# Two heads' transposed scores to one exponential of 1024 columns, in an attention between two mixtures of experts

## The chip, the cores and the metric

The kernel runs on 1 core of one Trainium2 chip. The metric is the device time of one execution in microseconds (us); times are medians of several runs.

## The reference

The reference is one layer: half a mixture of experts, attention, half a mixture of experts, on x of 4 x 512 tokens with 512 channels. The change touches the attention alone. For every batch and each of 16 heads of 32 channels:

```python
Xn = (X - mu) * jax.lax.rsqrt(var + LN_EPS) * ln_w + ln_b
Q, K, V = jnp.split(jnp.einsum('bsd,df->bsf', Xn, W_in), 3, axis=-1)
Q, K = (_rope(Q), _rope(K))
scores = jnp.einsum('bhqd,bhkd->bhqk', Q, K) / jnp.sqrt(jnp.float32(Dh))
probs = jax.nn.softmax(scores, axis=-1)
ctx = jnp.einsum('bhqk,bhkd->bhqd', probs, V)
out = jnp.einsum('bsd,df->bsf', ctx, W_out) + X
```

## The kernel before

One program feeds five engines, each with its own instruction stream in order: TensorE (PE), ScalarE (ACT), VectorE (DVE), GpSimd (POOL) and the DMA queue of SyncE (SP). The first expert stage runs to about 430 us of the span, attention to about 950 us, the second expert stage to the end.

Attention goes in 16 units (u = 0 to 15), four heads of one batch each. A unit's scores are computed twice. The first time (`pe_scores`, L445) queries lie on the partitions, one matmul of 512 columns for each head and each 128 queries. VectorE takes the row maximum (L1062), ScalarE writes the exponential in place and sums it (`act_scores`, L722: an ACTIVATE and then a read of the accumulator). The logarithm of that sum (L728) less the maximum is transposed (L452), copied (L1080, L1082) and placed by DMA (`fill`, L1350) as two extra rows of the stacked operand `St`. The second time (`pe_expo`, L465) keys lie on the partitions, the two extra rows subtract the logarithm, and ScalarE's exponential (`act_expo`, L735) gives the finished weights PT, which `pe_weigh` (L477) multiplies with V, four heads side by side, for 128 keys at a time.

All engines walk the same written order: for each u from -2 to 16, sixteen steps j = 0 to 15. At step j of unit u, TensorE issues, in this order:

- the first scores of unit u + 1. `scores_at` puts one in each step from 0 to 13, but two (numbers 5 and 6) in step 5 and two (10 and 11) in step 9. They use banks 4, 5 and 7 in turn, so number n waits (`a_den`) until ScalarE has summed number n - 3.
- the transposed scores number j - 3 of unit u (at steps 0 to 2 numbers 13 to 15 of unit u - 1). They use banks 2 and 3 in turn, so number n waits (`a_exp`) for exponential n - 2.
- in steps 0 to 5 a third of a projection for unit u + 2 (L434, four matmuls); in steps 7 to 9 and 11 to 13, where a unit has them, thirds of a value tile (L420) or of an output tile (L491, units 4, 5, 8, 9, 12 and 13); at steps 10, 14, 15 and 6 of the next unit, the four weighings of unit u.

ScalarE at step j does the exponential of the transposed scores first, and then those of the first scores; after these a cast of the projection (L715) at steps 5 and 8, and a tile's affine (L706, four ACTIVATEs) at step 6 (at 10 too in units 0 and 1, at neither from unit 10 on). L465, L445, L434 and L420 take their operands as fp32r; L477, L491, L271 and the fills L525 take plain fp32.

Unit 15 has no next unit: its steps hold the transposes (L271) and the router matmuls (L279) of the second expert stage. Before `fill` of unit 15, SP waits until all 240 transposed scores of units 0 to 14 have been issued (`a_ST`), and then issues five loads of the second expert stage.

Of the kernel before, what the change touches and what calls it, by code (L numbers as in the profile page):

```python
# [10 lines left out]
ACT = mybir.ActivationFunctionType  # L11
# [6 lines left out]
S = 512  # L18
NH = 16
DH = 32  # L20
# [47 lines left out]
def macaron_kernel(nc, X_in, ln_w, ln_b, W_in, W_out, gate_w, bias, w_gate, w_up, w_down,  # L68
# [4 lines left out]
    with ExitStack() as ctx:  # L73
# [20 lines left out]
        def bank(i):  # L94
            return ps[i // 2][:, i % 2, :]
# [19 lines left out]
        St = [at("St", AT + 16 * KB * j, [98, 2, 4, S], F32R) for j in range(3)]  # L115
        xT = [at("xT", AT + 48 * KB + 8 * KB * j, [128, 4, S], F32R) for j in range(2)]
        V = [at("V", AT + 64 * KB + 8 * KB * j, [128, 4, D]) for j in range(2)]
        PT = [at("PT", AT + 80 * KB + 2 * KB * j, [128, S]) for j in range(NP)]
        Y1 = at("Y1", AT + 16 * KB, [128, NT, D])
        HL = at("HL", AT + 104 * KB, [128, 4, S], F32R)  # L120
        o = AW + 36 * KB
# [333 lines left out]
        def pe_expo(e, u, j):  # L455
            d, hl, kt = St[u % 3], j % 4, j // 4
            n = 16 * u + j
            if j == 0:
                for h in range(4):
                    e.wait_ge(s_st[u % 3][h], 48 * (u // 3 + 1))  # L460
                e.wait_ge(s_m[u % 3], 32 * (u // 3 + 1))
                e.wait_ge(a_ones, 3)
            if n >= 2:
                e.wait_ge(a_exp, n - 1)
            e.matmul(bank(2 + j % 2), d[0:98, 1, hl, 128 * kt:128 * kt + 128], d[0:98, 0, hl, :],  # L465
                     start=True, stop=True).then_inc(a_ST, 1)

        def pe_weigh(e, u, kt):
            b = u // 4
            e.wait_ge(a_V, 4 * b + kt + 1)  # L470
            if kt == 0 and u:
                e.wait_ge(a_dr, u)
            for hl in range(4):
                n = 16 * u + 4 * kt + hl
                h = 4 * (u % 4) + hl
                e.wait_ge(a_exp, n + 1)
                t = e.matmul(bank(6)[32 * hl:32 * hl + 32, :], V[b % 2][:, kt, DH * h:DH * h + DH], PT[n % NP][:, :],  # L477
                             start=(kt == 0), stop=(kt == 3), tile_position=(0, 32 * hl), skip_group_check=True)
            t.then_inc(a_pv, 1)

# [46 lines left out]
        def pe_attention(e):  # L527
            for i in range(4):
                pe_atile(e, i)
            for u in range(-2, NU + 1):  # L530
                now, nxt, far, back = 0 <= u < NU, 0 <= u + 1 < NU, 0 <= u + 2 < NU, 0 <= u - 1 < NU
                new, val = new_tiles(u), new_values(u)
                if u == NU:
                    pe_logits(e, f2, 11)
                for j in range(16):
                    if u == NU - 1 and 2 <= j < 14:
                        pe_tile(e, f2, j - 2)
                    if u == NU - 1 and 6 <= j:
                        for i in {14: (8, 9), 15: (10,)}.get(j, (j - 6,)):
                            pe_logits(e, f2, i)  # L540
                    if nxt:
                        for s in scores_at(j):
                            pe_scores(e, u + 1, s)
                    if now and j >= 3:
                        pe_expo(e, u, j - 3)
                    if back and j < 3:
                        pe_expo(e, u - 1, j + 13)
                    if far and j < 6:
                        pe_project(e, u + 2, j // 3, j % 3)
                    if u == NU - 2 and j < 8 or u == NU - 1 and j < 3:  # L550
                        pe_fill(e)
                        pe_fill(e)
                    if u == -2 and j in (8, 9):
                        for third in range(3):
                            pe_value(e, j - 8, third)
                    if u == -1 and 8 <= j < 14:
                        pe_value(e, (j - 2) // 3, (j - 2) % 3)
                    if back and j == 6:
                        pe_weigh(e, u - 1, 3)
                    if u == NU and j == 6:  # L560
                        e.wait_ge(a_exp, 16 * NU)
                        pe_shared_up(e, f2, 0, (0,))
                    if j in T_AT[:len(new)]:
                        pe_atile(e, new[T_AT.index(j)])
                    for h, at_ in ((0, FIRST), (1, SECOND)):
                        if j in at_:
                            third = at_.index(j)
                            if val is not None:
                                pe_value(e, val + h, third)
                            if result_of(u, h) is not None:  # L570
                                pe_result(e, result_of(u, h), ((0, 1), (2,), (3,))[third])
                    if now and j == 10:
                        pe_weigh(e, u, 0)
                    if now and j == 14:
                        pe_weigh(e, u, 1)
                    if now and j == 15:
                        pe_weigh(e, u, 2)
                    if nxt and j == 15:
                        pe_rows(e, u + 1)
                    if u == NU and j in (8, 10, 12, 14):  # L580
                        pe_result(e, u - 4 + (j - 8) // 2)
# [147 lines left out]

        def act_expo(e, u, j):  # L730
            n = 16 * u + j
            e.wait_ge(a_ST, n + 1)
            if n >= NP:
                e.wait_ge(a_pv, (n - NP) // 4 + 1)
            e.activation(PT[n % NP][:, :], bank(2 + j % 2), ACT.Exp).then_inc(a_exp, 1)  # L735

        def act_attention(e):
            e.preload_act_table(ACT.Sqrt)
# [3 lines left out]
            for u in range(-2, NU + 1):  # L742
                now, nxt, far, back = 0 <= u < NU, 0 <= u + 1 < NU, 0 <= u + 2 < NU, 0 <= u - 1 < NU
                new = new_tiles(u)
                for j in range(16):
                    if u == NU - 2 and j == 9:
                        act_root(e, f2, 0)
                    if u == NU - 1 and 2 <= j < 14:
                        act_tile(e, f2, j - 2)
                    if now and j >= 3:  # L750
                        act_expo(e, u, j - 3)
                    if back and j < 3:
                        act_expo(e, u - 1, j + 13)
                    if nxt:
                        for s in scores_at(j):
                            act_scores(e, u + 1, s)
                    if far and j in S_AT:
                        act_split(e, u + 2, S_AT.index(j))
                    if u == -2 and j == 9:
                        act_stats(e, 1)  # L760
                        e.preload_act_table_set("natural_log_exp_and_others")
                    if j in T_AT[:len(new)]:
                        act_atile(e, new[T_AT.index(j)])
                    if nxt and j == 14:
                        act_log(e, u + 1)
# [684 lines left out]
```

## Time and profile before

| | |
|---|---|
| median of 3 runs | 1369.07 us (1364.05 to 1369.32) |
| the profiled execution | 1369.51 us, its span 1367.7 us |
| TensorE's granted clock, mean | 0.946 of full speed |
| PE busy over the span | 1189.1 us (87%) |
| ACT busy over the span | 512.9 us (37%) |
| DVE busy over the span | 622.5 us (46%) |

The mean over the span hides the stages: ScalarE is nearly idle in the expert stages and busy in attention. What bears on the change is the stretch from 500 to 926 us, and in it the order of time on TensorE and ScalarE.

### The profile page before, as it was taken

The page shows a single profiled execution, that of the slowest core. Times are in us where ns is not written, and L with a number is a line of the kernel's source. Part 1 is how long each engine was busy: PE and PEld are TensorE (multiplying, and loading weights), DVE is VectorE, ACT ScalarE, POOL GpSimd, SP SyncE. Part 2 cuts the span into 40 slices and gives each one's busy share as a digit, 9 for nine tenths or more (in the row PEclk, how much of TensorE's full clock was granted, in tenths as well). Part 3 has the DMA queues.
Part 4 walks back from the last instruction along what each step waited for, and adds up shares of the span by engine and source line. Part 5 has one row for each costly group of instructions (what it writes and reads, how often), then busy time and mean ns, then how long its engine had stood idle before and what let it go on. Part 6 is the DMA issues. An engine that isn't in the chain of part 4 may idle for free.

```text
span 1367.7 us, 25752 instructions
## 1 busy us (share of the span) xinstructions
PE 1189.1 (87%) x10130; PEld 758.6 (55%) x10130; DVE 622.5 (46%) x1130; ACT 512.9 (37%) x1297; POOL 509.6 (37%) x413
## 2 busy tenths in 40 slices
PE   7998998888892678999999999889998998888980
PEld 5535766566671554665565565464336766665650
DVE  6993222122224767677777776613980212221220
ACT  3312111111111268888788788742122111111100
POOL 0123455455552933233234233000304555454544
PEclk9999999999996788999999999999998999999995
DMA  9996999999978844433534533232845999999957
GB/s 348 348 404 213 313 342 339 339 338 324 331 168 227 261 108 105 98 101 97 144 82 106 155 81 88 65 131 92 324 171 169 337 344 343 337 341 332 322 84 134
DMA packets 146200, 307.27 MB, mean 225 GB/s; under 512 B 17568, under 2 KB 50720, under 8 KB 146080
## 3 DMA queue, kind: packets, MB, share of 16 engines
q1 hardware_dynamic: 112960, 238.32, 51.8%
q0 software_dynamic: 23808, 57.69, 18.4%
q10 hardware_dynamic: 9312, 9.62, 2.1%
q8 instruction: 81, 1.33, 0.4%
q14 instruction: 39, 0.32, 0.1%
HBM read 222.47 MB, written 61.87 MB: 208 GB/s over the span
## 4 chain that ended last, share of the span: by engine, by line
PE 50%; DMA 27%; DVE 11%; ACT 4%; issue 3%; POOL 3%; SPq 1%; DVEq 0%; POOLq 0%; ACTq 0%
DMA ya_d<-osb,tok 10%; DMA out<-osb,tok 10%; PE ps L369 9%; PE ps L385 5%; PE ps L434 5%; DMA buf<-xn_d,tok 4%; PE ps L477 4%; PE ps L465 4%; PE ps L445 4%; PE ps L491 4%; PE ps L317 2%; PE ps L316 2%; PE ps L420 2%; DVE osb L993 2%; PE ps L279 2%
## 5 line engine op out<-in xcount | busy, mean ns | idle before, releaser
L369 PE MATMUL ps<-bufT,gu 128*64 128x96 f32 x6144 | 298.1, 259 | 0.0
L369 PEld LDWEIGHTS ps<-bufT,gu 128*64 128x64 f32 x6144 | 287.6, 175 | 9.1 <-issue 2.5
L993 DVE TENSOR_SCALAR osb<-ps,gt 96x512 f32<-96x512 f32 x128 | 94.0, 746 | 283.7 <-PE ps L385 70.8
L1062 DVE TENSOR_REDUCE Mx<-ps 128x1 f32<-128x512 f32 x256 | 170.5, 684 | 79.3 <-PE ps L445 78.7
L682 ACT COPY bufT<-ps 128x384 f32<-128x384 f32 x128 | 61.0, 478 | 352.7 <-PE ps L352 352.6
L722 ACT ACTIVATE ps<-ps,Mx 128x512 f32<-128x512 f32 x256 | 175.7, 689 | 36.3 <-DVE Mx L1062 35.5
L385 PE MATMUL ps<-wd,h 64*96 64x512 f32 x768 | 180.4, 602 | 3.2 <-DVE osb L993 3.2
L735 ACT ACTIVATE PT<-ps 128x512 f32<-128x512 f32 x256 | 159.4, 623 | 57.4 <-PE ps L465 55.5
L1182 POOL DMA_INDIRECT buf<-xn_d,tok x128 | 128.0, 1000 | 96.5 <-issue 61.6
L445 PE MATMUL ps<-St 96*128 96x512 f32 x256 | 118.8, 480 | 18.6 <-ACT ps L722 15.7
L465 PE MATMUL ps<-St 98*128 98x512 f32 x256 | 112.0, 438 | 12.5 <-DMA St<-mh 8.2
L986 DVE TENSOR_TENSOR h<-sg,ps 128x288 f32<-128x288 f32 x64 | 29.1, 454 | 204.7 <-PE ps L369 204.7
L352 PE MATMUL ps<-cst,buf 96*128 96x96 f32 x512 | 67.9, 263 | 60.4 <-DMA buf<-xn_d,tok 58.8
L434 PE MATMUL ps<-xT,wqk 128*128 128x512 f32 x384 | 110.2, 413 | 5.9 <-DVE xT L1033 5.9
L352 PEld LDWEIGHTS ps<-cst,buf 96*128 96x128 f32 x512 | 47.2, 143 | 116.6 <-DMA buf<-xn_d,tok 69.3
L1227 POOL TENSOR_TENSOR t<-t,rp 128x512 f32<-128x512 f32 x32 | 41.2, 1286 | 187.4 <-DVE t L1047 185.7
L385 PEld LDWEIGHTS ps<-wd,h 64*96 64x96 f32 x768 | 58.8, 159 | 77.6 <-issue 71.8
L434 PEld LDWEIGHTS ps<-xT,wqk 128*128 128x128 f32 x384 | 76.9, 201 | 24.1 <-DVE xT L1033 6.3
L1218 POOL DMA_INDIRECT out<-osb,tok x32 | 46.1, 1439 | 108.3 <-DVE osb L993 69.0
L445 PEld LDWEIGHTS ps<-St 96*128 96x128 f32 x256 | 49.7, 194 | 64.2 <-ACT ps L722 33.4
L1218 POOL DMA_INDIRECT ya_d<-osb,tok x32 | 46.2, 1443 | 100.1 <-DVE osb L993 63.9
L465 PEld LDWEIGHTS ps<-St 98*128 98x128 f32 x256 | 49.9, 195 | 47.2 <-issue 22.1
(149 smaller groups left out, 1481.7 us busy)
## 6 DMA issues: line engine op xcount, KB each, us to landing
gu<-in_L_ffn_w_gate SPq DMA_DIRECT2D x64, 768.0 KB, 13.2
gu<-in_L_ffn_w_up SPq DMA_DIRECT2D x64, 768.0 KB, 15.5
wd<-in_L_ffn_w_down SPq DMA_DIRECT2D x64, 768.0 KB, 18.4
St<-HL SPq DMA_DIRECT2D x192, 128.0 KB, 2.3
wqk<-wp_d SPq DMA_DIRECT2D x32, 512.0 KB, 5.2
xn_d<-XN SPq DMA_DIRECT2D x24, 256.0 KB, 3.6
X<-in_L_attn_X SPq DMA_DIRECT2D x4, 1024.0 KB, 10.7
ya_d<-X SPq DMA_DIRECT2D x4, 1024.0 KB, 18.4
```

What stands on the lines that cost most here:

```text
L352: t = e.transpose(bank(x % 2)[:, CAP * c:CAP * c + CAP], f.buf[x % NB][:, 128 * c:128 * c + 128], cst[0:CAP, C_ID:C_ID + CAP])
L369: t = e.matmul(bk[64 * k:64 * k + 64, CAP * j:CAP * j + CAP], gu[:, 2 * k + m, c, j:F:3], f.bufT[(2 * q + k) % 4][:, c, :], start=(c == 0) ...
L385: t = e.matmul(bank(4 + k)[0:CAP, :], f.h[q % 2][p, CAP * j:CAP * j + CAP], wd[p, j, :], start=(j == 0), stop=(j == 2), tile_position=(64 ...
L434: t = e.matmul(bk, wqk[:, x, c, k, :], xT[y][:, c, :], start=(n == 0), stop=(n == 11))
L445: e.matmul(bank((4, 5, 7)[n % 3]), d[0:96, 0, hl, 128 * qt:128 * qt + 128], d[0:96, 1, hl, :], start=True, stop=True).then_inc(a_sc, 1)
L465: e.matmul(bank(2 + j % 2), d[0:98, 1, hl, 128 * kt:128 * kt + 128], d[0:98, 0, hl, :], start=True, stop=True).then_inc(a_ST, 1)
L722: e.activation(bk, bk, ACT.Exp, bias=Mx[:, qt, hl:hl + 1], accum_out=Dn[:, qt, hl:hl + 1]).then_inc(a_den, 1)
L735: e.activation(PT[n % NP][:, :], bank(2 + j % 2), ACT.Exp).then_inc(a_exp, 1)
L993: e.tensor_scalar(f.osb[x % 4][:, :], bank(4 + x % 2)[0:CAP, :], f.gt[:, x % 8:x % 8 + 1], None, ALU.mult).then_inc(f_ev, 1)
L1062: e.tensor_reduce(Mx[:, qt, hl:hl + 1], bank((4, 5, 7)[n % 3]), AX, ALU.max, negate=True).then_inc(a_max, 1)
L1182: e.indirect_dma_start(out=f.buf[x % NB][:, :], out_offset=None, in_=f.xn_d, in_offset=bass.IndirectOffsetOnAxis(ap=f.tok[:, x:x + 1], axi ...
L1218: e.indirect_dma_start(out=f.y[x % 2], out_offset=bass.IndirectOffsetOnAxis(ap=f.tok[:, x:x + 1], axis=0), in_=f.osb[x % 4][:, :], in_offs ...
```

## The change

Transposed scores are made for two neighbouring heads at one step, into banks 2 and 3, which are the two halves of `ps[1]`, and one ACTIVATE of 1024 columns turns both into weights. PT becomes four buffers of two heads instead of eight of one. The pair (0, 1) stands at step 3, (2, 3) at 5, and so on to (12, 13) at 15 and (14, 15) at step 1 of the next unit; even steps have none. A pair's two matmuls wait (`a_exp`) until the exponential of the pair before has ended.

```diff
--- before.py
+++ after.py
@@ -115,7 +115,7 @@
         St = [at("St", AT + 16 * KB * j, [98, 2, 4, S], F32R) for j in range(3)]
         xT = [at("xT", AT + 48 * KB + 8 * KB * j, [128, 4, S], F32R) for j in range(2)]
         V = [at("V", AT + 64 * KB + 8 * KB * j, [128, 4, D]) for j in range(2)]
-        PT = [at("PT", AT + 80 * KB + 2 * KB * j, [128, S]) for j in range(NP)]
+        PT = [at("PT", AT + 80 * KB + 4 * KB * j, [128, 2, S]) for j in range(NP // 2)]
         Y1 = at("Y1", AT + 16 * KB, [128, NT, D])
         HL = at("HL", AT + 104 * KB, [128, 4, S], F32R)
         o = AW + 36 * KB
@@ -460,10 +460,11 @@
                     e.wait_ge(s_st[u % 3][h], 48 * (u // 3 + 1))
                 e.wait_ge(s_m[u % 3], 32 * (u // 3 + 1))
                 e.wait_ge(a_ones, 3)
-            if n >= 2:
-                e.wait_ge(a_exp, n - 1)
-            e.matmul(bank(2 + j % 2), d[0:98, 1, hl, 128 * kt:128 * kt + 128], d[0:98, 0, hl, :],
-                     start=True, stop=True).then_inc(a_ST, 1)
+            if n:
+                e.wait_ge(a_exp, n // 2)
+            for k in range(2):
+                e.matmul(ps[1][:, k, :], d[0:98, 1, hl + k, 128 * kt:128 * kt + 128], d[0:98, 0, hl + k, :],
+                         start=True, stop=True).then_inc(a_ST, 1)
 
         def pe_weigh(e, u, kt):
             b = u // 4
@@ -473,8 +474,8 @@
             for hl in range(4):
                 n = 16 * u + 4 * kt + hl
                 h = 4 * (u % 4) + hl
-                e.wait_ge(a_exp, n + 1)
-                t = e.matmul(bank(6)[32 * hl:32 * hl + 32, :], V[b % 2][:, kt, DH * h:DH * h + DH], PT[n % NP][:, :],
+                e.wait_ge(a_exp, n // 2 + 1)
+                t = e.matmul(bank(6)[32 * hl:32 * hl + 32, :], V[b % 2][:, kt, DH * h:DH * h + DH], PT[n % NP // 2][:, n % 2, :],
                              start=(kt == 0), stop=(kt == 3), tile_position=(0, 32 * hl), skip_group_check=True)
             t.then_inc(a_pv, 1)
 
@@ -541,10 +542,10 @@
                     if nxt:
                         for s in scores_at(j):
                             pe_scores(e, u + 1, s)
-                    if now and j >= 3:
+                    if now and j >= 3 and j % 2:
                         pe_expo(e, u, j - 3)
-                    if back and j < 3:
-                        pe_expo(e, u - 1, j + 13)
+                    if back and j == 1:
+                        pe_expo(e, u - 1, 14)
                     if far and j < 6:
                         pe_project(e, u + 2, j // 3, j % 3)
                     if u == NU - 2 and j < 8 or u == NU - 1 and j < 3:
@@ -558,7 +559,7 @@
                     if back and j == 6:
                         pe_weigh(e, u - 1, 3)
                     if u == NU and j == 6:
-                        e.wait_ge(a_exp, 16 * NU)
+                        e.wait_ge(a_exp, 8 * NU)
                         pe_shared_up(e, f2, 0, (0,))
                     if j in T_AT[:len(new)]:
                         pe_atile(e, new[T_AT.index(j)])
@@ -729,10 +730,10 @@
 
         def act_expo(e, u, j):
             n = 16 * u + j
-            e.wait_ge(a_ST, n + 1)
+            e.wait_ge(a_ST, n + 2)
             if n >= NP:
                 e.wait_ge(a_pv, (n - NP) // 4 + 1)
-            e.activation(PT[n % NP][:, :], bank(2 + j % 2), ACT.Exp).then_inc(a_exp, 1)
+            e.activation(PT[n % NP // 2][:, :, :], ps[1][:, :, :], ACT.Exp).then_inc(a_exp, 1)
 
         def act_attention(e):
             e.preload_act_table(ACT.Sqrt)
@@ -747,10 +748,10 @@
                         act_root(e, f2, 0)
                     if u == NU - 1 and 2 <= j < 14:
                         act_tile(e, f2, j - 2)
-                    if now and j >= 3:
+                    if now and j >= 3 and j % 2:
                         act_expo(e, u, j - 3)
-                    if back and j < 3:
-                        act_expo(e, u - 1, j + 13)
+                    if back and j == 1:
+                        act_expo(e, u - 1, 14)
                     if nxt:
                         for s in scores_at(j):
                             act_scores(e, u + 1, s)
```

## Rows read from the trace of the kernel before

**Rows 1.** Windows of the whole core: PE, PEld, DVE, ACT, POOL busy us (count), PEclk, DMA share, GB/s.
```profile
440.00:561.00 121.00, 93.25 (x351) 60.18 (x352) 83.50 (x152) 71.68 (x183) 59.71 (x48) 0.82 0.54 154
561.00:892.00 331.00, 320.90 (x1459) 190.46 (x1458) 231.17 (x405) 271.83 (x683) 96.46 (x78) 0.99 0.41 103
```
**Rows 2.** Waits from 561 to 892: who waited for whom, total us, times, longest us.
```profile
PEld ps L445 <- ACT ps L722: 21.3, 28, 1.6
...
PEld ps L465 <- ACT PT L735: 12.6, 18, 1.7
```
**Rows 3.** Groups by line: ScalarE's 1024-column form; busy us, mean ns | idle before, releaser.
```profile
L639 ACT ACTIVATE sgs<-ps 128x1024 f32<-128x1024 f32 x8 | 8.2, 1024 | 65.8 <-PE ps L304 65.8
```
**Rows 4.** Timeline, ScalarE, unit 2, steps 5 to 8: start us, us, operation.
```profile
560.21 0.60 ACT L735 ACTIVATE PT<-ps 128x512 f32<-128x512 f32 x1
560.71 0.66 ACT L722 ACTIVATE ps<-ps,Mx 128x512 f32<-128x512 f32 x1
...
565.07 0.65 ACT L735 ACTIVATE PT<-ps 128x512 f32<-128x512 f32 x1
565.54 0.72 ACT L722 ACTIVATE ps<-ps,Mx 128x512 f32<-128x512 f32 x1
566.12 0.26 ACT L722 ACTIVATION_READ_ACCUMULATOR ps<-ps,Mx 128x1 f32 x1
```
**Rows 5.** Timeline, TensorE, unit 2: step 5 unstalled, step 9 stalled.
```profile
559.31 0.63 PE L445 MATMUL ps<-St 96*128 96x512 f32 x2
...
565.88 1.04 PE L445 MATMUL ps<-St 96*128 96x512 f32 x2
...
566.43 0.19 PEld L445 LDWEIGHTS ps<-St 96*128 96x128 f32 x1 [0.59 <-ACT ps L722]
```
**Rows 6.** Timeline, step 9 of units 4 and 13: the sum read, the second weight load.
```profile
616.33 0.27 ACT L722 ACTIVATION_READ_ACCUMULATOR ps<-ps,Mx 128x1 f32 x1
...
616.82 0.19 PEld L445 LDWEIGHTS ps<-St 96*128 96x128 f32 x1 [0.24 <-ACT ps L722]
...
847.51 0.24 ACT L722 ACTIVATION_READ_ACCUMULATOR ps<-ps,Mx 128x1 f32 x1
...
848.89 0.19 PEld L445 LDWEIGHTS ps<-St 96*128 96x128 f32 x1 [0.24 <-issue]
```
**Rows 7.** Timeline, unit 6: ScalarE late at step 5, TensorE stalled at step 9.
```profile
663.98 0.59 ACT L735 ACTIVATE PT<-ps 128x512 f32<-128x512 f32 x1
...
670.18 0.50 PE L445 MATMUL ps<-St 96*128 96x512 f32 x1 [0.49 <-ACT ps L722]
```
**Rows 8.** Timeline, TensorE, unit 5, steps 13 to 15.
```profile
650.48 1.02 PE L491 MATMUL ps<-wout,cT 128*128 128x512 f32 x2
650.94 0.80 PE L465 MATMUL ps<-St 98*128 98x512 f32 x1
651.67 1.06 PE L477 MATMUL ps<-PT,V 128*32 128x512 f32 x8
```
**Rows 9.** Timeline, unit 15, first steps: TensorE and SP's queue.
```profile
888.75 0.60 PE L465 MATMUL ps<-St 98*128 98x512 f32 x1
...
890.47 0.47 PE L465 MATMUL ps<-St 98*128 98x512 f32 x1
...
893.46 1.23 SPq L1350 DMA_DIRECT2D St<-mh  x2
...
897.73 0.77 PE L465 MATMUL ps<-St 98*128 98x512 f32 x1 [4.91 <-DMA St<-mh]
```
**Rows 10.** Timeline, units 15 and 16: the last exponentials and the last weighing.
```profile
914.67 0.48 PE L465 MATMUL ps<-St 98*128 98x512 f32 x1
914.99 0.60 PE L271 MATMUL ps<-cst,XN 128*128 128x128 f32 x4
...
922.88 0.71 PE L465 MATMUL ps<-St 98*128 98x512 f32 x2
...
925.22 0.14 PEld L477 LDWEIGHTS ps<-PT,V 128*32 128x32 f32 x2 [0.56 <-ACT PT L735]
```

## The prediction

> **What bounds the kernel now.** I read the busy windows first, then the waits, then the timelines of TensorE and ScalarE step by step. In the 331 us in which attention runs steadily, TensorE is busy 320.9 us at a granted share of 0.99, ScalarE 271.8 us [rows 1]. Two fp32r matmuls of 512 columns in a row take 0.63 us where a single one takes 0.40 [rows 5], so TensorE takes a new one every 0.23 us; the reader is to see that it is nearly always fed. Its waits are small: 21.3 us for ScalarE's sums of the first scores, 12.6 us put down to the exponentials PT [rows 2]. So ScalarE's total, 59 us short of the stretch, is not what sets the end; what counts is when it releases something to TensorE. One place stands out: step 9, where two first scores are issued. The second of them, number 11, needs the sum of number 8, which ScalarE makes at step 7. In unit 2 the two matmuls span 1.04 us instead of 0.63, 0.41 us of stall; the sum's read ends at 566.38, and the second one's weights load from 566.43 [rows 4, 5]. The same place stalls 0.49 us in unit 6 [rows 7].
>
> **ScalarE's saving.** It gives up 256 exponentials of 512 columns (0.60 us, as at 560.21) for 128 of 1024. In a row a single one lets the next instruction start after 0.50 or 0.47 us (560.21 to 560.71, 565.07 to 565.54) [rows 4]. The 1024-column form exists elsewhere in the kernel and takes 1.024 us, 0.42 more than 0.60 [rows 3, 4]. So a pair occupies about 0.48 + 0.42 = 0.90 us against 0.96 for two: 0.06 saved, 128 x 0.06 = 7.7 us in all. As TensorE is the full engine, I cost this gain at nothing, with 7.7 us as its other bound (a rival below). The Trainium skill ("ScalarE: Activation LUTs", section "What ACT_TABLE_LOAD costs") gives an ACTIVATE a fixed 186 ns, of which 93 ns overlap back to back. By that the saving would be 93 ns a pair, an estimate of 11.9 us in all; the rows here show two thirds of it.
>
> **Step 9, the main cost.** What ScalarE does from step 5 until the sum of score 8 changes order. Before: exponential 2, scores 5 and 6, cast, exponential 3, score 7, the affine, exponential 4, score 8. After: pair (2, 3), scores 5 and 6, cast, score 7, affine, pair (4, 5), score 8. Exponential 5 is now ahead of score 8. Two pairs (1.80) stand for three singles (0.50 + 0.48 + 0.47 = 1.45): 0.35 us later, in a stretch in which ScalarE has no pause. Where exponential 2 started as soon as its matmul ended, the pair also waits for the second matmul, 0.23 us: 0.58 us together. TensorE has issued the same number of matmuls before score 11 as before, so it arrives no later, and the delay becomes stall:
> - units 2 and 3 already stall there: 2 x 0.58 = 1.16 us.
> - units 4, 5, 8, 9: the read ends at 616.60, the weight load starts at 616.82, 0.22 us later, against 0.05 us in the stalled unit 2; 0.17 us of room: 4 x 0.41 = 1.64 us [rows 6].
> - units 6, 7, 10, 11: VectorE's statistics hold ScalarE back before step 5 (exponential 2 at 663.98 is not fresh from its matmul [rows 7]), so 0.35 each, or 0.3 in 10 and 11: 1.3 us.
> - units 12 and 13 have 1.14 us of room (847.75 to 848.89) [rows 6]: nothing.
> - units 0 and 1 run behind ScalarE from step 6 to 15, and seven pairs take no longer there than their fourteen singles: nothing. In unit 14 a later stall on score 12 takes it up: 0.3 us, at most 0.65.
>
> Sum 4.4 us. Score 13 waits at step 11 for score 10, made at step 9 behind pair (6, 7); TensorE by then is late by nearly as much, so only about 0.1 us more in units 5, 9, 10 and 11: 0.4 us. **Cost 4.8 us.** Its bounds: nothing, if the order of ScalarE gives way somewhere I do not see; 12 units x (0.58 + 0.42) = 12 us if step 11 stalls in full too.
>
> **The pair's own wait.** With both banks in one exponential, TensorE may not start a pair until the last has ended; what is queued behind it are the projection or value matmuls and the next first scores. The pairs are two steps apart, each some 1.4 us or more. Against before, the exponential ends 0.42 us later and begins 0.23 later. Pair (4, 5) of unit 2 would end about 566.3, and pair (6, 7) stands after the stalled score 11, at 567.0 or later [rows 4, 5]. It just fits: nothing, bounded above by 0.3 us for each of the twelve units of that place, 3.6 us. Weighings and the reuse of PT buffers come at the same or a later step than their new exponentials: no new wait.
>
> **What TensorE gains.**
> - Step 14 has no lone fp32r matmul between the output tile's and the weighing's fp32 ones. Before: 650.94 to 651.67, 0.73 us, of which the output matmul still needs 0.43 less 0.03; so 0.33 go and the matmul costs 0.23 at step 13 [rows 8]: 0.1 us in six units, 0.6 us.
> - Unit 15: a lone transposed score between fp32 ones takes 0.32 us (914.67 to 914.99) against 0.23 behind another, in seven steps: 0.6 us [rows 10].
> - The start of unit 15. TensorE stands idle for 4.91 us until the DMA of the two extra rows lands. SP issues it at 893.46, behind five loads that wait until transposed score 15 of unit 14, at 890.47, is done [rows 9]. This one moves from step 2 to step 1, beside number 14 (888.75 + 0.23 = 888.98): SP's whole queue, `fill` and the stores of the normalized tiles behind it, moves 1.49 us earlier, and nothing else was late for it. Gain 1.5 us.
> - The last weighing waits until exponential 15 lets its last head start at 925.22. Numbers 13 and 14 go out together at 922.88. After, 14 and 15 go out there, 0.23 us later for number 13 moved ahead: the second at 923.3, ended at 923.7, and 1.02 us of exponential end at 924.8 [rows 3, 10]: 0.4 us.
>
> **Gain 3.1 us.** Sum: 1369.5 (the profiled execution, 0.4 above the median of the runs shown) + 4.8 - 3.1 = 1371.2, against the median 1369.07 + 1.7 = 1370.8. I predict 1371 us. This case's own range: 1369.1 - 3.1 = 1366 to 1369.1 - 3.1 + 12 + 3.6 = 1381.6; its likely part ends near 1376.
>
> **Rivals.**
> - *The clock falls* (slower). From 440 to 561 us, where stalls are long (units 0 and 1), the granted share is 0.82, so a third of the time is spent at 1.2 GHz; from 561 to 892 it is 0.99 [rows 1]. If the added stalls (in unit 2 from 0.41 to 0.99 us at step 9) brought it to 0.95, 33 us would run at the lower level and lose 16 us: 1387 us. Against it: unit 6 has stalls now and the share stays at 0.99. It decides once half-speed pieces show after 561. Beside it stands the Trainium skill, "TensorE: Matmul & The Clock Gate", section "A second HAM failure mode: psum-queue depth-cycling": small idles between matmul groups that cycle through PSUM can make the clock oscillate. No row here shows it past 561 us; by it this change, which adds such idles, would speak for this rival. Chance 0.13.
> - *ScalarE was the limit after all* (faster). If the stalls of 21.3 and 12.6 us [rows 2] come of ScalarE's sum of work rather than its order, the 7.7 us come through with the 3.1: 1358 us. For it: those waits exist in nearly every unit. Against it: ScalarE is busy only 271.8 of 331 us [rows 1]. It decides if step 9's stall does not grow. Chance 0.12.
> - *The pair's wait binds* (slower, a ping-pong between one pair of banks and ScalarE): 112 steady pairs x 0.1 us = 11 us, less the gains: 1377 us. Against it: in unit 2 exponential 4 ended at 565.72 (565.07 + 0.65), and the next matmul on its bank came after score 11, loaded at 566.43 [rows 4, 5]. Chance 0.07.
>
> My forecast has 0.68.
>
> **How the numbers follow.** About 0.5% (6.8 us) is what a measurement of this kernel tells from no change: 1362.3 to 1375.9. My case puts 0.62 within it, 0.05 above and 0.01 below. The clock rival is slower, 0.13; the pair's wait gives 0.03 slower, 0.04 same; ScalarE's gives 0.11 faster, 0.01 same. Together: faster 0.12, same 0.67, slower 0.21. The range for 8 in 10 leaves out most of the clock rival and half of the faster one: 1361 to 1379.
>
> **What would show it.** In the profile after: L735 x128 of about 1.03 us; step 9's two first scores spanning about 1.6 us instead of 1.04 in unit 2; ScalarE's waits for TensorE longer than before, its busy time less by about 30 us (overlapping records count the start-up twice); the idle before the first transposed score of unit 15 still some 5 us, but the whole place 1.5 us earlier against its neighbours; PEclk 0.99 from 561 on. I am wrong if step 9 does not stall more, if new idles stand before L465 put down to L735 in steady units, or if half-speed pieces appear.

## The result, and the profile after

| | before | after |
|---|---|---|
| median of 17 runs each | 1370.04 us (1364.05 to 1377.05) | 1379.22 us (1371.58 to 1391.81) |
| the profiled execution | 1369.51 us, span 1367.7 | 1377.9 us, span 1376.0 |
| TensorE's granted clock, mean | 0.946 | 0.947 |

The ratio is 1.0078, with a 95% interval of 1.0055 to 1.0101: 9.2 us slower, where I had forecast 1 to 2 us. It lies just above my range (1361 to 1379). Ratios and their intervals, here and below, rest on the runs in the faster of the chip's two states alone and medians on all runs, so a ratio is not the quotient of two medians.

The first view is the table of windows; the second row answers to the second of [rows 1].
```profile
440.00:561.00 121.00, 89.26 (x336) 57.78 (x337) 81.04 (x146) 67.08 (x159) 56.76 (x46) 0.80 0.57 166
561.00:892.00 331.00, 316.38 (x1435) 188.58 (x1433) 231.15 (x397) 264.11 (x574) 98.73 (x80) 1.00 0.41 103
```
The clock stands at 1.00 throughout the steady stretch. TensorE is busy 4.5 us less and has issued 24 matmuls fewer in the same 331 us: it is late, not slowed. The groups by line show ScalarE's new form, and the waits from 561 to 892 answer to [rows 2].
```profile
L736 ACT ACTIVATE PT<-ps 128x1024 f32<-128x1024 f32 x128 | 131.6, 1028 | 35.4 <-PE ps L466 33.5
```
```profile
ACT ps L723 <- DVE Mx L1063: 50.7, 43, 2.5
PEld ps L445 <- ACT ps L723: 27.7, 30, 1.7
```
The pair takes 1028 ns. TensorE's waits for the sums of first scores grew from 21.3 us to 27.7.

The unit is the right ruler, since neighbouring units of a kind (2 and 3, 12 and 13) repeat to 0.1 us. I measured it on the trace of each kernel from one unit's transposes (L452) to the next one's; "twelve steady units" are 2 to 13. Units 14 and 15 end where the second shared expert starts (L296).

| us | units 0, 1 | units 2 to 13 | units 14, 15 | L296 to the second experts | second experts |
|---|---|---|---|---|---|
| before | 58.97 | 308.03 | 66.49 | 111.6 | 329.9 |
| after | 60.00 | 316.12 | 65.33 | 110.8 | 326.3 |

So 8.1 of the 8.3 us by which the span grew lie in the twelve steady units. (The first score starts 3.7 us later after, and the second expert stage, which the change does not touch, is 3.6 us shorter; these two cancel.) Step by step, the 8.1 us are 1.4 until step 5, 3.6 at step 9 (the second of its first scores, number 11), 3.75 from there to score 13 at step 11, and -0.7 in the rest. In this split a transposed score that moved to a later step is counted at its old place, with 0.23 us: without that, the starts up to step 5 come 1.4 us earlier, as 12 x 0.23 = 2.8 us of matmuls now stand behind them.

**Step 9, unit 2.** TensorE, its weight loads and ScalarE, answering to [rows 4, 5]:
```profile
571.57 0.39 PE L445 MATMUL ps<-St 96*128 96x512 f32 x1
572.74 0.50 PE L445 MATMUL ps<-St 96*128 96x512 f32 x1 [0.78 <-ACT ps L723]
```
```profile
570.96 1.06 ACT L736 ACTIVATE PT<-ps 128x1024 f32<-128x1024 f32 x1
571.87 0.70 ACT L723 ACTIVATE ps<-ps,Mx 128x512 f32<-128x512 f32 x1
572.43 0.26 ACT L723 ACTIVATION_READ_ACCUMULATOR ps<-ps,Mx 128x1 f32 x1
```
The two starts are 1.17 us apart, where they were 0.55 apart before (565.88 to 566.43 [rows 5]): 0.62 more, and I had said 0.58.

**Step 11, unit 5.** This is the loss that I had costed at almost nothing. Before, ScalarE and then TensorE from the pass over score 9 to the load for score 13:
```profile
643.82 0.66 ACT L722 ACTIVATE ps<-ps,Mx 128x512 f32<-128x512 f32 x1 [0.98 <-DVE Mx L1062]
644.41 0.19 ACT L722 ACTIVATION_READ_ACCUMULATOR ps<-ps,Mx 128x1 f32 x1
644.50 0.61 ACT L715 CAST HL<-HL 128x512 fp32r<-128x512 f32 x1
645.01 0.60 ACT L735 ACTIVATE PT<-ps 128x512 f32<-128x512 f32 x1
645.50 0.66 ACT L722 ACTIVATE ps<-ps,Mx 128x512 f32<-128x512 f32 x1
...
646.38 0.19 PEld L445 LDWEIGHTS ps<-St 96*128 96x128 f32 x1 [0.84 <-ACT ps L722]
```
After:
```profile
652.04 0.66 ACT L723 ACTIVATE ps<-ps,Mx 128x512 f32<-128x512 f32 x1 [1.53 <-DVE Mx L1063]
...
652.71 0.61 ACT L716 CAST HL<-HL 128x512 fp32r<-128x512 f32 x1
653.22 1.02 ACT L736 ACTIVATE PT<-ps 128x1024 f32<-128x1024 f32 x1
654.14 0.66 ACT L723 ACTIVATE ps<-ps,Mx 128x512 f32<-128x512 f32 x1
...
654.97 0.19 PEld L445 LDWEIGHTS ps<-St 96*128 96x128 f32 x1 [1.45 <-ACT ps L723]
```
Score 9's own matmul starts at 640.83 before and 648.64 after. From it to ScalarE's pass over score 9 is 2.99 us before and 3.40 after; from there to the load for score 13 it is 2.56 and 2.93. The second difference, 0.37, is the wide exponential (0.92 against 0.49 until the next instruction). The first, 0.41, is VectorE's maximum, which ScalarE waits for. The cause is one step further back, on VectorE beside GpSimd. Before:
```profile
640.68 0.82 DVE L1031 CAST xT<-xF 128x512 fp32r<-128x512 f32 x1
641.54 1.65 DVE L1033 TENSOR_TENSOR xT<-xF,xT 128x512 fp32r<-128x512 f32 x1
643.11 1.87 DVE L1062 TENSOR_REDUCE Mx<-ps 128x1 f32<-128x512 f32 x3
...
638.71 1.28 POOL L1234 TENSOR_TENSOR HL<-HL 128x512 fp32r<-128x512 f32 x1 [1.93 <-ACT HL L715]
639.95 1.27 POOL L1227 TENSOR_TENSOR t<-t,rp 128x512 f32<-128x512 f32 x1
```
After:
```profile
648.26 1.46 DVE L1032 CAST xT<-xF 128x512 fp32r<-128x512 f32 x1
...
651.32 1.87 DVE L1063 TENSOR_REDUCE Mx<-ps 128x1 f32<-128x512 f32 x3
...
646.93 1.27 POOL L1235 TENSOR_TENSOR HL<-HL 128x512 fp32r<-128x512 f32 x1 [3.07 <-ACT HL L716]
648.16 1.27 POOL L1228 TENSOR_TENSOR t<-t,rp 128x512 f32<-128x512 f32 x1
```
The cast ends 0.29 us behind GpSimd's multiplication in both (641.22 to 641.51, 649.43 to 649.72), however long it has been under way. GpSimd is later because it waited longer for ScalarE's cast of HL (3.07 us against 1.93, for the operation ahead of the multiplication). The same cast takes 0.41 us where GpSimd has nothing under way as it starts.

### The profile page after: what moved, and what is told of

Read it like the earlier page. It is cut to its first block, busy times and chain, and to the rows that moved or that the text cites. A ratio compares the mean times of both kernels' runs of the same rounds, so it can differ in the third digit from the quotient of the medians.

```text
span 1376.0 us, 25500 instructions
## 1 busy us (share of the span) xinstructions
PE 1203.8 (87%) x10130; PEld 767.2 (56%) x10130; DVE 625.6 (45%) x1130; ACT 505.0 (37%) x1169; POOL 508.5 (37%) x413
## 4 chain that ended last, share of the span: by engine, by line
PE 44%; DMA 29%; DVE 9%; issue 6%; ACT 5%; POOL 4%; SPq 1%; POOLq 0%; DVEq 0%; ACTq 0%
DMA ya_d<-osb,tok 11%; DMA out<-osb,tok 9%; PE ps L369 7%; DMA buf<-xn_d,tok 6%; PE ps L434 5%; PE ps L385 4%; PE ps L466 4%; PE ps L478 3%; PE ps L445 3%; PE ps L492 3%; PE ps L279 2%; PE ps L420 2%; PE ps L317 2%; ACT ps L723 2%; PE ps L316 2%
## 5 line engine op out<-in xcount | busy, mean ns | idle before, releaser
L369 PE MATMUL ps<-bufT,gu 128*64 128x96 f32 x6144 | 309.1, 258 | 8.8 <-issue 8.3
L369 PEld LDWEIGHTS ps<-bufT,gu 128*64 128x64 f32 x6144 | 291.7, 174 | 24.6 <-issue 16.4
L723 ACT ACTIVATE ps<-ps,Mx 128x512 f32<-128x512 f32 x256 | 170.5, 668 | 68.3 <-DVE Mx L1063 68.2
L736 ACT ACTIVATE PT<-ps 128x1024 f32<-128x1024 f32 x128 | 131.6, 1028 | 35.4 <-PE ps L466 33.5
L466 PE MATMUL ps<-St 98*128 98x512 f32 x256 | 87.3, 422 | 12.9 <-DMA St<-mh 6.2
L692 ACT ACTIVATE sg<-ps 128x288 f32<-128x288 f32 x64 | 26.3, 411 | 154.6 <-PE ps L369 123.9
```

The source lines that it names most:

```text
L369: t = e.matmul(bk[64 * k:64 * k + 64, CAP * j:CAP * j + CAP], gu[:, 2 * k + m, c, j:F:3], f.bufT[(2 * q + k) % 4][:, c, :], start=(c == 0) ...
L466: e.matmul(ps[1][:, k, :], d[0:98, 1, hl + k, 128 * kt:128 * kt + 128], d[0:98, 0, hl + k, :], start=True, stop=True).then_inc(a_ST, 1)
L723: e.activation(bk, bk, ACT.Exp, bias=Mx[:, qt, hl:hl + 1], accum_out=Dn[:, qt, hl:hl + 1]).then_inc(a_den, 1)
L736: e.activation(PT[n % NP // 2][:, :, :], ps[1][:, :, :], ACT.Exp).then_inc(a_exp, 1)
```

## The experiments

Each ratio is to the kernel before, measured beside it, with its 95% interval. In the diffs a minus is a line of the kernel named first.

**e1, e2: a sum ahead of the pair.** e1 is the kernel after with ScalarE's order turned at step 7, e2 at every odd step.
```diff
+                    late = j == 7
+                    if nxt and late:
+                        for s in scores_at(j):
+                            act_scores(e, u + 1, s)
                     if now and j >= 3 and j % 2:
                         act_expo(e, u, j - 3)
                     if back and j == 1:
                         act_expo(e, u - 1, 14)
-                    if nxt:
+                    if nxt and not late:
```
(e1. In e2 `late` is `j % 2 == 1`.)

> The changed kernel, but at step 7 alone ScalarE sums first score 8 before the pair's exponential. Theory A (ScalarE's order: the pair ahead of the sum makes TensorE stall at step 9): the stall before score 11 at step 9 goes in units 1 to 11 (0.6 us in units 1, 2, 3, 6, 7, 0.2 in the others, 4.5 us in all), so about 4 us less than the changed kernel: ratio to the kernel before about 1.004. Theory B (the pair's own wait for one pair of banks): the pair (4, 5) now ends 0.66 us later, so its successor waits longer and the time rises or stays: 1.008 or more. Theory C (the clock, or the place elsewhere): no change, 1.008, and a step 9 as long as in the changed kernel.

> The changed kernel, but at every odd step ScalarE does the first scores before the pair. Theory A: also the stall before score 13 at step 11 goes (0.3 to 0.6 us in six units, 2.8 us in all), 7 us less than the changed kernel: ratio to before about 1.002 to 1.003. Theory B: worse than the changed kernel, as each exponential ends 0.66 us later (1.3 at steps 5 and 9) and the next pair waits for it: over 1.010. Theory C: 1.008.

e1: median 1376.69 us, ratio 1.0064 [1.0039, 1.0088]; units 2 to 13 took 314.8 us, 1.3 less than after, where I had expected some 4. e2: 1384.74 us, 1.0114 [1.0093, 1.0136]; 323.6 us. In e1 step 9's stall is gone, -1.3 us against before where after has +3.6, but 7.3 us come back by step 11 where after has 3.75. The weight loads of unit 2 show where: right behind score 11 stands the pair (6, 7), which now waits for exponential (4, 5).
```profile
570.96 0.19 PEld L445 LDWEIGHTS ps<-St 96*128 96x128 f32 x1 [0.29 <-ACT ps L723]
571.87 0.30 PEld L466 LDWEIGHTS ps<-St 98*128 98x128 f32 x2 [0.73 <-ACT PT L736]
```
So both releases come from one ScalarE queue that is late, and its order only chooses which of them TensorE waits for. e2, where every odd step does this, loses 7.5 us more than after, and the waits of the pairs' weight loads for the exponential before grow from 10.1 us in 12 places to 28.2 in 40 (561 to 892 us): the pair's wait for the pair before, which I costed at nothing, has no room to spare.

**e3: no wide instruction.** The kernel before, with two single exponentials, on their own two banks, in each slot of a pair.
```diff
-                    if now and j >= 3:
+                    if now and j >= 3 and j % 2:
                         pe_expo(e, u, j - 3)
+                        pe_expo(e, u, j - 2)
...
-                    if now and j >= 3:
+                    if now and j >= 3 and j % 2:
                         act_expo(e, u, j - 3)
+                        act_expo(e, u, j - 2)
...
```
(Numbers 14 and 15 stand in the same way at step 1 of the next unit.)

> The kernel before, but with transposed scores and their exponentials two at a time at the odd steps, each exponential still 512 columns of a bank of its own. Theory A (placement, not width): the same loss as the changed kernel, ratio 1.007 to 1.010. Theory B (the wide instruction on one pair of banks): the loss goes, 0.998 to 1.002, as the first bank is free 0.5 us earlier. Theory C: 1.000 to 1.008, without step 9 to explain it.

Median 1376.18 us, ratio 1.0038 [1.0008, 1.0069]; units 2 to 13 took 315.8 us, after 316.1. By steps its loss is that of after: +3.3 at step 9, +3.5 to step 11. In the steady units the loss belongs to the odd steps, not to the 1024-column instruction or its two banks. (Its median is 3 us below after's and its ratio 1.0038 against 1.0078, its steady units are not shorter; the difference lies outside them and stays open.)

**e8: the delay alone.** The kernel before with two unused copies of 128 columns on ScalarE at step 7, ahead of score 8's sum, and nothing else.
```diff
+                    if nxt and now and j == 7:
+                        for k in range(2):
...
+                            e.copy(idle_[:, 128 * k:128 * k + 128], cst[:, 0:128]).then_inc(a_idle, 1)
```


> The kernel before with two copies of 128 columns on ScalarE at step 7 of each unit, ahead of the sum of score 8; nothing reads them. They take some 0.35 us together, what the pair adds to ScalarE there. Theory A (what matters is that ScalarE's sum of score 8 comes later): score 11 at step 9 stalls 0.3 to 0.4 us more in units 2, 3, 6 and 7 and 0.1 to 0.2 in 4, 5, 8 and 9, twelve steady units 2 to 3 us longer (310 to 311 us). Theory B (the paired wait is needed for the loss): no change, 308 us.

Median 1370.89 us, ratio 1.0001 [0.9974, 1.0029]; units 2 to 13 took 309.4 us, 1.4 more than before, where I had expected 2 to 3. At step 9 it adds 0.40 us in units 2, 3, 6 and 7, nothing in 12 and 13, nothing in 4, 5, 8 and 9 (I had expected 0.1 to 0.2), and 0.26 in 10 and 11. So the step-9 wait answers one for one to ScalarE's delay where it stood before. But my room for units 4, 5, 8 and 9 was wrong: I had taken 0.17 us, up to the weight load of score 11, and it reaches to the matmul. In unit 4 score 11's matmul starts 0.63 us behind score 10's before and 0.65 in e8, though the sum's read ends 0.41 us later (0.19 and 0.60 behind it) and the load waits for it:
```profile
619.28 0.19 PEld L447 LDWEIGHTS ps<-St 96*128 96x128 f32 x1 [0.48 <-ACT ps L724]
```
The room was 0.4 us. In units 10 and 11 the 0.26 us are not lost: score 13 starts as long behind score 10 as before (3.58 us), since it waits there for a sum that has not moved. A stall is taken up where a later wait stands whose release does not hang on it.

**e4, e6: the pairs one step later.** e4 puts the pair (0, 1) at step 4, (2, 3) at 6 and so on to (12, 13) at 0 and (14, 15) at 2; e6 leaves the first two at 3 and 5.
```diff
-                    if now and j >= 3 and j % 2:
-                        pe_expo(e, u, j - 3)
-                    if back and j == 1:
-                        pe_expo(e, u - 1, 14)
+                    if now and j >= 4 and j % 2 == 0:
+                        pe_expo(e, u, j - 4)
+                    if back and j in (0, 2):
+                        pe_expo(e, u - 1, j + 12)
```
(The same on ScalarE.)

> The changed kernel with its pairs at the even steps (4, 6, ... 14, and 0 and 2 of the next unit) instead of the odd ones. Theory A: no pair stands ahead of the sum of score 8 at step 7 or those of 10 and 11 at step 9, and the two extra rows have one more step to land before the first pair: the stalls at steps 9 and 11 fall to those of the kernel before or less, and the wait at step 3 (0.4 us a unit in the changed kernel) goes; unit 15 loses its 1.4 us. About 12 us less than the changed kernel: ratio 0.997 to 1.001. Theory B: as the changed kernel, 1.008. Theory C: 1.008.

> As e4_even, but the first two pairs stay at steps 3 and 5, as in the changed kernel; the others at 8, 10, 12, 14, 0 and 2. It splits the 10.2 us between the changed kernel's and e4_even's twelve steady units (316.1 and 305.9). Theory A' (the wait at step 3 for the DMA of the two rows has its part, the rest is steps 9 and 11): 308 to 310 us, the first scores of steps 4 on about 0.4 later than in e4_even, no stall added at steps 9 and 11. If the first two pairs were the cause: 314 us or more. If they cost nothing: 306.

e4: units 2 to 13 took 305.9 us, 2.1 less than before and 10.2 less than after. e6: 311.3 us, between, and above the 308 to 310 that I had expected. At step 9 both have less stall than before (-2.0 us). But e4's median is 1378.96 us, ratio 1.0051 [1.0019, 1.0084], and e6's 1378.91, 1.0054 [1.0032, 1.0077]. In e4's profile the stretch from L296 to the second expert stage takes 126.2 us instead of 111.6. TensorE, and then the windows there:
```profile
983.61 1.97 PE L325 MATMUL ps<-cst,R 128*128 128x128 f32 x8 [3.85 <-DVE R L943]
```
```profile
960.00:982.00 22.00, 19.64 (x60) 6.81 (x58) 21.56 (x70) 2.05 (x2) 4.68 (x2) 1.00 1.03 407
982.00:1019.60 37.60, 35.99 (x43) 10.76 (x44) 26.84 (x34) 4.78 (x8) 7.63 (x3) 0.50 0.19 73
1019.60:1040.00 20.40, 20.40 (x52) 6.72 (x51) 8.31 (x14) 3.73 (x6) 0.00 (x0) 1.00 0.56 195
```
Behind an idle stretch of 3.85 us (before 1.8, after 2.2 at the same place) the granted clock stood at 0.50, that is 1.2 GHz, for 37.6 us, though TensorE was then busy 36 of them. The five other profiles with 2.9 to 3.2 us of idle there (e2, e3, e6, e10, e12) have 3.4 us at that level behind it. So this does not explain e6: its stretch takes 113.1 us, its steady units 3.3 us more than before, and the rest of the 8 us by which its median stands above before's stays open.

**e5, e9, e11, e10: the idle stretch filled.** Six unused matmuls of 272 columns ahead of the second router's keys (L325), in after (e5), in e4's kernel (e9) and in before (e11); e10 is after once more, on the same chip as e9 and e11.
```diff
-            e.wait_ge(f_step, 21 * f.n + R_KEY)
-
             e.wait_ge(f_hs, 4 * f.n + 2)
+            if f.n:
+                for _ in range(6):
+                    e.matmul(bank(7)[:, 0:C_N], ident, cst[:, :], start=True, stop=True)
+            e.wait_ge(f_step, 21 * f.n + R_KEY)
```


> The changed kernel with six unused matmuls (272 columns, into a bank that is free) on TensorE right before the second router's keys, where it stands idle 2 to 4 us for VectorE in every profile so far, and where the clock fell for 37.6 us in the profile of e4_even. They compute nothing that is used. Theory D (the spread of the changed kernel's times is this fall of the clock, and the steady loss is the placement): attention's twelve steady units still take 316 us, but runs with a granted share at or below 0.938 disappear and the median falls by 3 to 8 us, ratio 1.003 to 1.007. If the clock there has nothing to do with it: spread and median as the changed kernel's, 1.008.

> The kernel after the change with pairs at steps 4, 6, 8, 10, 12, 14, 0 and 2 (as e4), and six unused fills of TensorE before the second router's keys (as e5); SP's order as before. Theory placement: the twelve steady units take about 306 us (before 308.0, after 316.1), as in e4 and e7. Theory clock at the keys: e4's 15 us between the last attention stage's L296 and the second expert stage came of a granted clock that fell to half behind 3.85 us of idle TensorE, so with the fills that stretch takes 111 to 113 us (e4 126.2) and no half-speed piece stands behind the keys; median 1369 to 1372 us, ratio to before 0.997 to 1.001. Rival: the 15 us belong to e4's order of attention and not to the idle stretch: then that stretch stays at 120 us or more and the median near 1379.

> The kernel before with nothing changed but the six unused fills of TensorE before the second router's keys: what they cost or give by themselves. Before waits 1.83 us there, so the fills (six matmuls, a few tenths of a us each) fit in the wait: ratio 0.998 to 1.001, median 1368 to 1371. If the fills themselves saved time in every kernel, the ratio here would be below 0.998, and a gain of e9 would be theirs and not that of the even steps.

> The kernel after the change once more, on the same chip as e9 and e11. Expected: median 1377 to 1381 us, ratio 1.0055 to 1.010; units 2 to 13 about 316 us in its profile, 8 us more than before, with score 13's wait for the sum of score 10 at step 11 in units 4, 5 and 8 to 13 and score 11's wait at step 9 in units 2 to 11. If it came out within 0.3% of before, the slowdown would not belong to the kernel.

| | median us | ratio to before | units 2 to 13 | L296 to second experts |
|---|---|---|---|---|
| e5, after + fills | 1379.07 | 1.0059 [1.0034, 1.0083] | 316.2 | 111.0 |
| e9, even steps + fills | 1366.55 | 0.9986 [0.9961, 1.0012] | 306.8 | 111.2 |
| e11, before + fills | 1370.92 | 1.0018 [1.0001, 1.0035] | 307.8 | 112.4 |
| e10, after | 1378.53 | 1.0092 [1.0060, 1.0124] | 316.4 | 111.5 |

e9 against e4 takes back the 15 us; in e5 and e11, where nothing had fallen there, the fills give nothing (I had expected 3 to 8 us of e5). Five of e4's nine runs had a mean granted clock of 0.933 to 0.935, and none of e9's twelve had less than 0.948. So e4's loss was the clock behind the idle stretch. e9 has the lowest median of the study. It and e10 ran on one chip, 12 us apart; to before it can't be told apart. One reason lies at the end of attention: units 14 and 15 took 67.3 us in e9 and 65.2 in e11, with 6.8 us at half clock in both, so between these two profiles the pairs at even steps lose 2.1 us there and gain 1.0 in the steady units. Which wait that is I did not trace.

**e7: SP's order too.** e9 with `fill` of unit 15 issued before the five loads.
```diff
-                if u == NU - 1:
-                    e.wait_ge(a_ST, 16 * (NU - 1))
-                    load_router(e, f2)
-                    load_shared(e, f2)
                 for j in range(16):
...
                         fill(e, u)
+                    if u == NU - 1 and j == 0:
+                        e.wait_ge(a_ST, 16 * (NU - 1))
+                        load_router(e, f2)
+                        load_shared(e, f2)
```


> e4_even with the six fills before the keys, and with SP issuing unit 15's two rows ahead of the second expert stage's five loads. Theory D: twelve steady units at 306 us as in e4_even, unit 15 3 to 4 us shorter, since the 4.9 us wait for the two rows at its start goes, and no fall of the clock before the keys: ratio 0.993 to 0.997, faster than both kernels. If the clock falls elsewhere instead: 1.000 to 1.005.

Median 1371.78 us, ratio 1.0021 [0.9995, 1.0046], where I had expected 0.993 to 0.997; units 2 to 13 took 306.6 us, and units 14 and 15 69.6, not less than e9's 67.3. TensorE's wait for the two rows is gone, but one as long stands behind it:
```profile
897.90 1.12 PE L271 MATMUL ps<-cst,XN 128*128 128x128 f32 x4 [5.03 <-DVE XN L836]
```
VectorE in turn waited 10.1 us for the stores of XN, which are still queued behind the loads.

**e12: VectorE's held cast.** The kernel after, with one of VectorE's slots moved.
```diff
-        S_AT, T_AT, H_AT = (5, 8), (6, 10), (7, 9, 11, 13)
+        S_AT, T_AT, H_AT = (5, 8), (6, 10), (8, 9, 11, 13)
```


> The kernel after the change, with one thing moved on VectorE: in units 1, 5 and 9 the first cast and subtraction of a new batch's halves (xT) stand at step 8, behind the row maximum of score 9, instead of at step 7 ahead of it. Theory of the held cast: in unit 5 the cast takes 1.46 us after the change and 0.82 before, and in both it ends 0.29 us behind the GpSimd multiplication beside it; GpSimd is late since ScalarE's cast of HL is late; so the maximum of score 9, its sum and the sum of score 10 come 0.4 us later than by the wide exponential alone. With the cast moved, ScalarE's pass over score 9 starts about 1.3 us or more earlier against its matmul (3.40 us after it now), the wait of score 13 at step 11 in units 5 and 9 goes (0.6 us each), and these units take 27.3 to 27.5 us (27.97 and 27.67 after, 26.47 before); units 2 to 13 about 315 us (316.1 after). Rival: the 0.6 us of step 11 are the wide exponential alone, ahead of score 10's sum: then units 5 and 9 stay within 0.15 us of after. The median moves by about 1 us, less than it can tell.

Unit 5 took 26.74 us (after 27.97, before 26.47), unit 9 26.25 (after 27.67, before 26.47); the other ten stayed within 0.1 us. Units 2 to 13 took 313.7 us. Median 1375.11, ratio 1.0029 [0.9997, 1.0062]. ScalarE's pass over score 9 starts 1.71 us behind its matmul instead of 3.40. VectorE, and GpSimd's operation beside the cast:
```profile
649.50 0.98 DVE L1032 CAST xT<-xF 128x512 fp32r<-128x512 f32 x1
650.51 0.69 DVE L1034 TENSOR_TENSOR xT<-xF,xT 128x512 fp32r<-128x512 f32 x1
...
648.93 1.27 POOL L1231 TENSOR_TENSOR HL<-HL,t 128x512 f32<-128x512 f32 x1
```
The cast again ends 0.28 us behind GpSimd, and the subtraction, 1.65 us long where GpSimd worked beside it, takes 0.69. The gain is twice what I expected, as the waits of both score 12 (step 10) and score 13 went. The rival, that only the wide exponential delays score 13 there, is out. e12 does not say how much of the 0.8 us is the cast's: before has the held cast too, moving it there was not tried, and unit 9 now takes 0.2 us less than before.

## Why the prediction was wrong, point by point

- **What bounds the kernel: right.** TensorE's waits for ScalarE at fixed places set the time, not ScalarE's sum. ScalarE's saving came (busy 505.0 us after, 512.9 before: 7.9 us, as the sum of 7.7 had it, and not the "about 30 us" of my list of signs) and bought nothing; the rival "ScalarE was the limit" is refuted.
- **Step 9: the wait right, the total partly by luck.** 4.1 us forecast for units 2 to 13, 3.6 measured. Units 2 and 3 lost 0.6 each, as said, 10 and 11 0.2 (0.3 said), 12 and 13 nothing. But 4, 5, 8 and 9 lost 0.2 each where I had 0.41, as their room was 0.4 and not 0.17 (e8), and 6 and 7 lost 0.6 where I had 0.35: the sum's read there ends 0.60 us later, as in units 2 and 3. The two errors nearly cancel.
- **Step 11: this step failed.** I wrote that TensorE "by then is late by nearly as much" and took 0.4 us; it cost 3.75. Measured from score 10's own matmul, the end of its sum came 0.5 to 0.6 us later in units 2 to 4 and 6 to 8, 0.8 to 0.9 in 10 and 11, and 1.1 in 5, 9, 12 and 13. TensorE's lateness of step 9 does count against this, and in units 2, 3, 6 and 7, where it was 0.6 us, nothing was added. Elsewhere it was 0.2 or nothing, and what the delay exceeds it by, and by the room that score 13 had (0.8 us in 12 and 13, at most 0.1 in 5, 9, 10 and 11), is the cost: 0.8 us each in 5 and 9, 0.6 in 10 and 11, 0.3 in 12 and 13. (0.1 in 4 and 8 I did not trace.) Of the delay 0.42 is the wider exponential, which my bound had (0.42 in each unit); the rest is ScalarE's later start on it, which I had nowhere.
- **In units 12 and 13 I had looked at step 9's room alone.** Score 13's load stood 0.83 us behind its release before, and 0.05 after. Before, the single exponential 5 of step 8 filled a pause; after, ScalarE stands idle there, and does both halves ahead of score 10's sum:
```profile
836.40 0.66 ACT L723 ACTIVATE ps<-ps,Mx 128x512 f32<-128x512 f32 x1 [0.60 <-DVE Mx L1063]
836.99 0.19 ACT L723 ACTIVATION_READ_ACCUMULATOR ps<-ps,Mx 128x1 f32 x1
837.50 0.62 ACT L716 CAST HL<-HL 128x512 fp32r<-128x512 f32 x1 [0.32 <-POOL HL L1231]
838.03 1.02 ACT L736 ACTIVATE PT<-ps 128x1024 f32<-128x1024 f32 x1
```
- **GpSimd and VectorE: not in the sum at all.** ScalarE's later cast of HL held GpSimd, GpSimd held VectorE's cast, and that held ScalarE: by the trace 0.41 us in units 5 and 9, half of their 0.8. In units 10 to 13 the same delay comes back to ScalarE without VectorE: its next cast of HL waits for GpSimd, in unit 10 1.07 us where before had 0.54, and in units 12 and 13 0.32 where before had nothing. Unit 10, before and then after:
```profile
775.01 0.62 ACT L715 CAST HL<-HL 128x512 fp32r<-128x512 f32 x1 [0.54 <-POOL HL L1230]
775.54 0.59 ACT L735 ACTIVATE PT<-ps 128x512 f32<-128x512 f32 x1
...
786.38 0.62 ACT L716 CAST HL<-HL 128x512 fp32r<-128x512 f32 x1 [1.07 <-POOL HL L1231]
786.90 1.02 ACT L736 ACTIVATE PT<-ps 128x1024 f32<-128x1024 f32 x1
```
No run moves GpSimd alone, so its share in units 10 to 13 is read from the trace and not tested.
- **Step 3: not in the sum.** TensorE comes to the first pair with one transposed score less behind it, 0.23 us earlier, and waits for the DMA of the two rows, which land when they did. That is 0.2 us in most units, 1.4 in all. I had looked for such a wait in unit 15 alone.
- **Step 14's credit (0.6 us): not there.** In unit 5 the output tile's last two matmuls and the weighing are 0.95 us apart (659.31 to 660.26) against 1.19 [rows 8]: 0.24 saved, and the matmul costs 0.23 at step 13.
```profile
659.31 1.02 PE L492 MATMUL ps<-wout,cT 128*128 128x512 f32 x2
660.26 1.06 PE L478 MATMUL ps<-PT,V 128*32 128x512 f32 x8
```
- **Unit 15's start: the way forecast, its worth open.** The first transposed scores come 1.45 us earlier behind unit 15's transposes (9.97 against 11.42), as I had said, and the wait for the two rows fell from 4.91 us [rows 9] to 3.51, where I had said it would stay near 5. In e8 and e11 it was 4.5 to 4.6 us, in e5 and e10 4.3 and 3.4.
```profile
908.85 1.19 PE L466 MATMUL ps<-St 98*128 98x512 f32 x2 [3.51 <-DMA St<-mh]
```
Units 14 and 15 together took 65.1 to 66.5 us in before, e8 and e11 and 62.5 to 65.3 in after, e5 and e10, a mean of 65.6 against 63.7: 1.9 us, where I had 2.5 of credits less 0.3 of unit 14. But pieces at half clock, of 6.8 to 10.2 us in the first three and 3.4 to 10.2 in the others, lie in them, so its size stays open.
- **The last weighing: as forecast.** Its second half starts 1.83 us behind the last transposed scores (936.07 to 937.90) where before has 2.34 [rows 10]; I had counted 1.9.
```profile
936.07 0.71 PE L466 MATMUL ps<-St 98*128 98x512 f32 x2
...
937.90 0.14 PEld L478 LDWEIGHTS ps<-PT,V 128*32 128x32 f32 x4 [1.04 <-ACT PT L736]
```
- **Units 0 and 1: costed at nothing.** They took 57.4 to 59.3 us in before, e8 and e11 and 59.0 to 61.3 in after, e5 and e10, some 1 to 2 us more. With 17 to 24 us of them at half clock I can't say by which wait.
- **The pair's own wait: nothing, as taken,** but only just (e1, e2).
- **The clock: right for this change** (1.00 in the steady stretch), and refuted as its rival; it fell in e4 instead, elsewhere.

The costs of units 2 to 13 are 1.4 + 3.6 + 3.75 = 8.8 us, less 0.7 that I did not trace: 8.1. I had 4.5 less 0.6 there, 3.9. These 4.2 us are the part of my error of 7.5 (9.2 against 1.7) that the runs show. Of the rest, 1.0 is in units 0 and 1 and 1.0 in units 14 and 15 of these two profiles; what is left lies between a median and one profile.

Open: what remains of the credits in units 14 and 15, what units 0 and 1 wait for, why e3's median is lower than its steady units say and e6's higher, and how much of step 11 goes if GpSimd and VectorE are kept out of it.

## What to carry to other kernels

Where engines walk one written order, cost a moved step at every release behind it, not at the first that stalls. At each, take how much later it comes, less the room in front of it, less the stall already taken. The stall at step 9 covered step 11 where it was as large as the delay there (units 2, 3, 6 and 7) and left the rest where it was 0 to 0.25 us against 0.8 to 1.1. Coupling two operations costs less by doing the pair at the later of the two places than at the earlier, since the earlier puts work ahead of a sum that is waited for (10 us between e4 and after, one step apart). Follow a late cast through the engines that seem idle: here it went ScalarE, GpSimd, VectorE, ScalarE, TensorE.

## What the runs showed of the hardware

- A VectorE cast of 512 columns takes 0.41 to 0.43 us alone. In unit 5 it starts with a GpSimd operation on two tensors under way, takes 0.57 to 1.48 us, and ends 0.28 to 0.29 us behind that operation in all fourteen profiles. The Trainium skill ("SBUF — State Buffer", section "SBUF: two separate sides") calls the pair of ports that the two engines share an exclusive lock, held for the whole instruction; the traces agree, by the 0.28 to 0.29 us. I had not looked for it, as VectorE was busy 46% and GpSimd 37%.
- After 3.85 us of idle TensorE the granted clock stood at 0.50 for 37.6 us of nearly unbroken matmuls (e4); after 2.9 to 3.2 us at the same place, for 3.4 us (e2, e3, e6, e10, e12); after 1.8 to 2.2, not at all there (before, after, e1, e8). Stalls of up to 1.3 us in the steady units after the change (step 9 of unit 6, where the two first scores start 1.49 us apart) left it at 1.00.
